# Two attention layers and their feed-forward parts on one Trainium2 core: the second attention's weighted sums in eight slots instead of nine

## The reference, cut to what matters

```python
x = L0(x, ctx)     # 8 heads of 16, then a relu feed-forward part
x = L1(x, ctx)     # 16 heads of 32; what follows is this layer
q  = layernorm(q_x, ...) @ Wq.T
kv = layernorm(kv_x, ...) @ Wkv.T
k, v = kv[0], kv[1]
attn = softmax(einsum('bhqd,bhkd->bhqk', q, k) * scale)
out  = einsum('bhqk,bhkd->bhqd', attn, v)
x = q_x + out @ Wo.T + bo
h = silu(x @ W1.T + b1)
x = x + h @ W2.T + b2
```

## Time and profile before

| | us |
|---|---|
| median of 3 runs (lowest, highest) | 5515.28 (5510.59, 5517.87) |
| the profiled execution's own time | 5516.99 |
| its span, first to last instruction | 5515.2 |
| PE busy in the span | 5316.3 (96%) |
| DVE busy | 4010.2 (73%) |
| ACT busy | 3172.4 (58%) |
| POOL busy | 2345.2 (43%) |

### The profile page before, as it was taken

How to read it: one execution, slowest core, us unless ns; L and a number is a source line. 1 busy time by engine, 2 the same in 40 slices (tenths; PEclk the granted TensorE clock), 3 DMA queues, 4 the chain that set the end, 5 groups by cost and what they waited for, 6 DMA issues and landing times. The chain is left out here.

```text
span 5515.2 us, 93900 instructions
## 1 busy us (share of the span) xinstructions
PE 5316.3 (96%) x28684; PEld 3344.6 (61%) x28684; DVE 4010.2 (73%) x6936; ACT 3172.4 (58%) x5792; POOL 2345.2 (43%) x1165
## 2 busy tenths in 40 slices
PE   8999999999799899999999999999999996999999
PEld 6744444444477565666666666656666663777777
DVE  6689999999477788888888888888888886332331
ACT  4268888888433466666666666666666663322222
POOL 0000000000000488888888888888888885000000
PEclk9989999999799899999999999999999998999999
DMA  7521111111333311111111111111111112322220
GB/s 216 130 48 38 38 38 38 38 38 31 111 120 115 101 40 30 41 39 42 41 28 41 41 42 40 28 42 41 39 42 28 41 28 62 120 87 69 92 84 23
DMA packets 329592, 324.44 MB, mean 59 GB/s; under 512 B 185744, under 2 KB 193808, under 8 KB 327184
## 3 DMA queue, kind: packets, MB, share of 16 engines
q1 hardware_dynamic: 329232, 319.92, 21.9%
HBM read 219.18 MB, written 100.53 MB: 58 GB/s over the span
## 5 line engine op out<-in xcount | busy, mean ns | idle before, releaser
L444 DVE TENSOR_REDUCE a_maxes<-a_mscore 128x1 f32<-128x458 f32 (+4 forms) x5376 | 3038.1, 624 | 590.5 <-PE a_mscore L502 559.1
L427 ACT ACTIVATE a_prob<-a_score 128x512 f32<-128x512 f32 x4992 | 2635.3, 598 | 1175.1 <-PE a_score L511 1162.1
L511 PE MATMUL a_score<-a_q,a_k 97*128 97x512 f32 (+1 forms) x4992 | 1980.2, 432 | 10.9 <-ACT a_prob L427 7.7
L502 PE MATMUL a_mscore<-a_k,a_qm 96*128 96x458 f32 (+4 forms) x5376 | 1893.1, 415 | 36.0 <-DMA a_k<-k 34.4
L530 PE MATMUL a_acc<-a_prob,a_v 128*32 128x512 f32 x9984 | 1601.0, 604 | 0.0
L502 PEld LDWEIGHTS a_mscore<-a_k,a_qm 96*128 96x128 f32 (+1 forms) x5376 | 1475.7, 310 | 159.9 <-DVE a_maxes L444 48.6
L393 POOL TENSOR_TENSOR a_added<-a_added,a_prob 128x1024 f32<-128x1024 f32 x640 | 1534.4, 2397 | 71.0
L511 PEld LDWEIGHTS a_score<-a_q,a_k 97*128 97x128 f32 (+1 forms) x4992 | 917.9, 193 | 970.7 <-ACT a_prob L427 525.5
L525 PE MATMUL a_acc<-a_prob,a_ones 128*1 128x512 f32 x2048 | 961.0, 591 | 0.0
L292 POOL MEMSET a_k<- 32x126 f32 (+4 forms) x6 | 6.3, 1053 | 1819.8 <-POOLq L60 1819.5
L530 PEld LDWEIGHTS a_acc<-a_prob,a_v 128*32 128x32 f32 x9984 | 292.5, 109 | 299.9 <-issue 154.7
(11 more groups left out here) (205 smaller groups left out, 3983.4 us busy)
## 6 DMA issues: line engine op xcount, KB each, us to landing
a_qm<-q SPq DMA_DIRECT2D x384, 64.0 KB, 1.9
a_q<-q SPq DMA_DIRECT2D x384, 64.0 KB, 1.9
acc<-a_acc_sb SPq DMA_DIRECT2D x384, 64.0 KB
e_part<-acc SPq DMA_DIRECT2D x90, 256.0 KB, 3.4
a_k<-k SPq DMA_DIRECT2D x48, 416.0 KB, 6.2
q<-m_qout SPq DMA_DIRECT2D x128, 128.0 KB, 2.3
e_wo<-wo_split SPq DMA_DIRECT2D x32, 512.0 KB, 4.3
k<-kv_k1out SPq DMA_DIRECT2D x24, 512.0 KB, 2.9
```

The source lines that it names most:

```text
L427: act.activation(prob[:, t], score[SCORES[it.j][t]][:], ACT.Exp, scale=SCALE).then_inc(exp_done, 1)
L444: dve.tensor_reduce(maxes[j][:, t, c:c + 1], mscore[u % UNIT_BANKS][:, 0:wide], AX.X, ALU.max).then_inc(unit_read, 1)
L502: pe.matmul(mscore[u % UNIT_BANKS][:, 0:wide], qm[j][r:r + ROW, t:NB:NB // P], kt[kk][r:r + ROW, at:at + wide], start=True, stop=True).the ...
L511: pe.matmul(score[SCORES[it.j][t]][:], kt[it.k][r:r + C, i * P:(i + 1) * P], qt[it.j][r:r + C, :], start=True, stop=True).then_inc(score_d ...
```

## The change

a1's tables are new. Tiles 0 to 7 fill two slots with values in all four column groups. Column group 3 of these two slots holds values, is copied out on its own (`side`, `copy_side` on ACT before exponential 20) and stored as a fourth partial result, so `SIDE` is 4. Six slots of three tiles each follow, whose column group 3 adds up the denominators of tiles 8, 9, 23 and 24, of the last tile (now all 128 rows, with ones only where there are keys), and `total`. That makes eight slots in four batches of two, in steps 17 and 22 of the item and in steps 9 and 13 of the next. DVE sums tiles 2 to 4 and 5 to 7, each in two pieces of 256 columns, in steps 9, 10, 17 and 19. POOL starts with tiles 10 and 11, adds both sums of DVE at once (1024 columns), and folds last. The table of units is new, and the weights are split from step 0 of the last item on. In `ending` each piece has three additions instead of two, the additions and splits for blocks 2 to 7 (counted from 0) are at other steps, piece 0 of a block is loaded one block earlier, and the last `attended` and `add_x` come one step later.

```diff
-            self.ROWS, self.SIDE, self.SUMS = 128, 3, 1
-            self.slots = [[(0, 3 * i), (1, 3 * i + 1), (2, 3 * i + 2), (3, ("one", 3 * i))] for i in range(8)]
-            self.slots.append([(0, 24), (1, 25), (3, ("sum", None))])
-            self.batches = [[0, 1], [2, 3], [4, 5], [6, 7], [8]]
-            self.at = {3: (3, True), 9: (4, True), 14: (0, False), 19: (1, False), 25: (2, False)}
-            self.copy_at = 5
+            self.ROWS, self.SIDE, self.SUMS = 128, 4, 1
+            self.slots = [[(c, 4 * i + c) for c in range(4)] for i in range(2)]
+            for i in range(2, 8):
+                first = 8 + 3 * (i - 2)
+                what = [("one", 8), ("one", 9), ("one", 23), ("one", 24), ("rest", 25), ("sum", None)][i - 2]
+                self.slots.append([(0, first), (1, first + 1), (2, first + 2), (3, what)])
+            self.batches = [[0, 1], [2, 3], [4, 5], [6, 7]]
+            self.at = {9: (2, True), 13: (3, True), 17: (0, False), 22: (1, False)}
+            self.copy_at, self.side_at = 14, 20
+            self.sum_at = (9, 10, 17, 19)
             self.CHUNKS, self.early = 7, 10
-            more = dict(enumerate([2, 1, 1, 0, 1, 2, 1, 1, 1, 0, 1, 2, 1, 1, 1, 1, 1, 2, 1, 1, 1, 1, 2, 1, 1, 0]))
+            more = dict(enumerate([1, 1, 1, 0, 2, 1, 2, 0, 1, 1, 2, 1, 1, 0, 1, 1, 2, 1, 2, 0, 2, 1, 1, 1, 2, 0]))
             self.FIRST, self.WIDTHS = [0], [SPAD]
...
-        self.closes = [max(ts) for ts in tiles]
+        summed = [[t[1] for i in b for _, t in self.slots[i] if isinstance(t, tuple) and t[0] != "sum"]
+                  for b in self.batches]
+        self.closes = [max(ts + ones) for ts, ones in zip(tiles, summed)]
...
-ADDS = 9
-ON_VECTOR, PIECES = range(22, 25), 4
-READ_BY = 7
+ADDS, READ_BY, SUMS_READ = 9, (1, 2, 5, 7), 8
+ON_VECTOR, PIECES = (range(2, 5), range(5, 8)), 2
+VSUMS = len(ON_VECTOR) * PIECES
...
-            ones = sb("ones", [P, 1], F32)
+            ones = sb("ones", [P, 2], F32)
             added, total = sb("added", [P, 2, NB], F32), sb("total", [P, NB], F32)
-            vsum = sb("vsum", [P, NB], F32)
+            vsum, side = sb("vsum", [P, 2, NB], F32), sb("side", [P, NB], F32)
...
-        SPLIT_AT = 4
+        SPLIT_AT = 0
...
-                for i in range(SIDE):
+                for i in range(ATEND):
                     sp.dma_start(acc_out[i, bass.ds(h * hd, hd), cols],
                                  acc_sb[j][i * 32:i * 32 + hd, :]).then_inc(acc_stored[j], 16)
+                if APART:
+                    sp.wait_ge(side_copied, n + 1)
+                    sp.dma_start(acc_out[ATEND, bass.ds(h * hd, hd), cols], side[3 * 32:P, :]).then_inc(side_stored, 16)
...
-                for i in range(1, 7):
-                    pool.wait_ge(exp_done, it.n * ST + 3 * i + 3)
-                    if i == 1:
+                for i, t in enumerate((10, 12, 14, 16, 18, 20)):
+                    pool.wait_ge(exp_done, it.n * ST + t + 2)
+                    if i == 0:
                         if not it.first:
                             pool.wait_ge(add_done, base)
-                        pool.tensor_tensor(added[:], prob[:, 1:3], prob[:, 4:6], ALU.add).then_inc(add_done, 1)
+                        pool.tensor_tensor(added[:], prob[:, 0:2], prob[:, 10:12], ALU.add).then_inc(add_done, 1)
                     else:
-                        pool.wait_ge(add_done, base + i - 1)
-                        pool.tensor_tensor(added[:], added[:], prob[:, 3 * i + 1:3 * i + 3],
-                                           ALU.add).then_inc(add_done, 1)
-                pool.wait_ge(exp_done, it.n * ST + ST)
+                        pool.wait_ge(add_done, base + i)
+                        pool.tensor_tensor(added[:], added[:], prob[:, t:t + 2], ALU.add).then_inc(add_done, 1)
+                pool.wait_ge(exp_done, it.n * ST + 23)
                 pool.wait_ge(add_done, base + 6)
-                pool.tensor_tensor(added[0:LAST_KEYS, 1], added[0:LAST_KEYS, 1], prob[0:LAST_KEYS, 25],
-                                   ALU.add).then_inc(add_done, 1)
+                pool.tensor_tensor(added[:, 0], added[:, 0], prob[:, 22], ALU.add).then_inc(add_done, 1)
+                pool.wait_ge(vsum_done, it.n * VSUMS + VSUMS)
                 pool.wait_ge(add_done, base + 7)
+                pool.tensor_tensor(added[:], added[:], vsum[:], ALU.add).then_inc(add_done, 1)
+                pool.wait_ge(add_done, base + 8)
                 if not it.first:
                     pool.wait_ge(pv_done, it.n * NBATCH)
                 pool.tensor_tensor(total[:], added[:, 0], added[:, 1], ALU.add).then_inc(add_done, 1)
-                pool.wait_ge(add_done, base + 8)
-                pool.wait_ge(vsum_done, it.n * PIECES + PIECES)
-                pool.tensor_tensor(total[:], total[:], vsum[:], ALU.add).then_inc(add_done, 1)
...
-                        last = min(max(L.batches[b][-1], 1), READ_BY - 1)
-                        act.wait_ge(add_done, it.n * ADDS - ADDS + (last if b < NBATCH - 1 else READ_BY))
-                if APART and t == ON_VECTOR[0] and not it.first:
-                    act.wait_ge(vsum_done, it.n * PIECES)
+                        act.wait_ge(add_done, it.n * ADDS - ADDS + READ_BY[b])
+                if APART and t == ON_VECTOR[0][0] and not it.first:
+                    act.wait_ge(vsum_done, it.n * VSUMS)
                 act.activation(prob[:, t], score[SCORES[it.j][t]][:], ACT.Exp, scale=SCALE).then_inc(exp_done, 1)
+            def copy_side(n):
+                act.wait_ge(pv_done, n * NBATCH + 1)
+                act.wait_ge(side_stored, n * 16)
+                act.activation(side[3 * 32:P, :], acc[3 * 32:P, :], ACT.Copy).then_inc(side_copied, 1)
             for it in items(act):
-                for s in range(GROUPS):
-                    if s == L.copy_at and not it.first:
+                for t in range(ST):
+                    if t == L.copy_at and not it.first:
                         copy_acc(it.n - 1, 1 - it.j, it.prev_use)
-                    exp(it, 2 * s)
-                    exp(it, 2 * s + 1)
+                    if APART and t == L.side_at:
+                        copy_side(it.n)
+                    exp(it, t)
...
-                    dve.wait_ge(exp_done, n * ST + ON_VECTOR[-1] + 1)
-                    dve.wait_ge(add_done, n * ADDS)
+                    dve.wait_ge(exp_done, n * ST + tiles[-1] + 1)
+                    if which == 0 and not first:
+                        dve.wait_ge(add_done, n * ADDS - ADDS + SUMS_READ)
                 cols = slice(i * NB // PIECES, (i + 1) * NB // PIECES)
-                dve.tensor_reduce(vsum[:, cols], prob[:, ON_VECTOR[0]:ON_VECTOR[-1] + 1, cols].rearrange("p t c -> p c t"),
+                dve.tensor_reduce(vsum[:, which, cols], prob[:, tiles[0]:tiles[-1] + 1, cols].rearrange("p t c -> p c t"),
...
-                    if APART and t < PIECES and not it.first:
-                        add_up(it.n - 1, t)
-                if APART and it.last:
-                    for i in range(PIECES):
-                        add_up(it.n, i)
+                    if APART and t in L.sum_at:
+                        add_up(it.n, it.first, *divmod(L.sum_at.index(t), PIECES))
...
+                if b == 1 and APART:
+                    pe.wait_ge(side_copied, n + 1)
...
+                            col = 1 if what[0] == "rest" else 0
...
-    SUM_AT, HALF_AT, A_AT, ADD_AT = (1, 3, 5, 7), (2, 4, 6, 8), (10, 11, 12, 13), (11, 12, 13, 14)
+    SUM_AT = [(1, 3, 5, 7)] + [(0, 3, 6, 9)] * (BLOCKS - 1)
+    HALF_AT = [(2, 4, 6, 8)] + [(1, 4, 7, 10)] * (BLOCKS - 1)
+    A_AT, ADD_AT = (11, 12, 13, 14), (12, 13, 14, 15)
...
-                    for k in range(KT) if n > 0 else ():
+                    for k in range(1, KT) if n > 0 else ():
                         next_acc(n + 1, k)
                     for d in range(KT):
                         load_wo(n + 1, d)
+                if n + 2 < BLOCKS:
+                    next_acc(n + 2, 0)
...
```

52 lines of the change are left out of this document (32 added, 20 removed).

## The result

The changed kernel takes 5428.08 us (median of 4 runs, 5424.27 to 5431.30), the kernel before 5512.93 in 4 runs beside it (5502.76 to 5517.87). The ratio is 0.9848, with a 95% interval of 0.9831 to 0.9865: 85 us faster. The prediction said 5410, in a range of 5375 to 5455.

A forecast was written before the change was run, and what follows sets the result against it. PE bounds a1: 21.66 - 1.20 - 0.18 + 0.52 = 20.80 us an item. 126 x 0.86 = 108.4, first item 1 more, a1's end costing 4, `ending` giving 0.5: 106 us less, 5410, range 5375 to 5455.

The forecast's parts named there:

- One batch less: In each a1 item, dropping the single-slot batch saves 1.20 us, and two waits ahead of it another 0.18.
- The long run: In a1, 13 scores and units between the batches of steps 22 and 9: bank waits start score 9 0.52 us late.
- The item: One a1 item goes from 21.66 to 20.80 us, a gain of 0.86.
- DVE and POOL: In an a1 item, sums of 0.95 us give DVE 19.0 us of work; POOL's 20.6 fits by 0.2.
- rival (c): In a1, DVE's sums slow POOL's additions as the splits do: item 22.2 us, 5590 us in all; chance 0.07.
- (a): In a1, the 13-score run waits for nothing and POOL's 20.6 us sets the item: 5382 us; chance 0.13.
- (b): In a1, the 13-score run goes at DVE's pace, losing 0.9 us: item 21.15 us, 5453 us; chance 0.15.
- (d): In a1, the wait only shifts, the seam losing three times 0.52 us: nothing gained, about 5515 us; chance 0.05.
- The end of a1: From item 126's first exponential to POOL's last addition: 59.2 us instead of 55.1, 4 us more.
- `ending`: After a1: 10.3 us gained from six waits, 5 lost at seven seams, 4.8 in its opening; net 0.5 gained.
- The first item: In a1, the first item has no old batches to finish and gives 1 us more gain.
- The opening: Start of the ending code: one more addition of 0.71 us and one more load for each of four pieces, 4.8 lost.

The follow-up runs named there:

- experiment 2: The changed kernel with its second batch cut in two, so five batches for the eight slots, slot 3 alone at step 25: 5431.46 us, ratio 0.9852.
- experiment 4: The changed kernel without the matmuls that add up the denominators of tiles 8, 9, 23, 24 and 25: 5420.47 us, ratio 0.9833.
- experiment 1: The changed kernel with a1's score banks reordered in odd items, so score 0 takes the bank of score 23, not 24: 5405.08 us, ratio 0.9803.
- experiments 5 and 6: The changed kernel, ending's code alone altered: additions of blocks 2 to 7 one step earlier (5412.02 us), or tables and load order as before the change (5445.60 us).

## Why the prediction was right, point by point

**One batch less** (1.20 an item). In the mean over all items of the kernel before, the single-slot batch lies in 1.30 us from score to score. The prediction took off 0.21 for the two scores without it, but 0.21 is a score behind a unit; a score right behind a score starts 0.235 later. With the 0.10 for the slower start the batch was worth 1.16. The two waits ahead of it cost 0.175 (predicted 0.18). The split of the 1.16 matters: 0.87 is the slot, and the 0.29 for the batch is mostly taken back by ACT (experiment 2). That a matmul in the fourth column group costs nothing beside the others is shown (experiment 4), and so is that values there cost what ones do: the batch of step 17, with values in all four groups, adds 1.95 us to its step, and the three others 1.93 to 1.94.

**The long run** (0.52). The mechanism was right, and the sum came out by luck: its terms were wrong both ways. Score 9 comes 6.06 us after score 23 in the mean, 5.54 of them PE's own pace (counted from the same gaps where nothing waits), so 0.52 are lost, as predicted. But score 0 waits 0.25 and not 0.35, since it starts 0.10 behind the exponential that frees its bank and not 0.15, and score 4 waits 0.08 and not 0.17. Left out was the slower start of PE behind each of the two waits, 0.34 from score to unit instead of 0.24, which the prediction had counted behind batches: 0.19 for both.

**The item** (20.80, measured 20.893). The missing 0.09 is 12 of the 18 us by which the prediction missed. 0.04 of it are the batch's price and the waits ahead of it, above. Another 0.04 lie in the new table of units, which the prediction put at nothing: two more steps than before have no unit and two more have two. Two scores are 0.235 apart without a unit between them, 0.447 with one and 0.68 with two, so each such pair of steps takes 0.02 longer than two steps with one unit each (the means of score-to-score times in steps without a wait).

**DVE and POOL.** The sums are 0.94 apart (1.03 long), predicted 0.95. DVE kept up. POOL's pause is 0.7 where I had 0.2, since its additions follow each other more closely (2.47) than I took; its work of an item is 20.2 us, not 20.6. They kept their 2.39 beside sums, as at 2913.27, where this row of DVE starts together with POOL's addition shown above, and in the mean of the page's group (the last number but the wait):

```profile
2913.27 1.03 DVE L482 TENSOR_REDUCE a_vsum<-a_prob 128x256 f32<-128x768 f32 x1
...
L410 POOL TENSOR_TENSOR a_added<-a_added,a_prob 128x1024 f32<-128x1024 f32 x640 | 1533.7, 2396 | 71.0
```

So rival (c) is refuted: what the split does to POOL a reduction doesn't do. The rule of the Trainium skill that the prediction cited ("SBUF — State Buffer", Who interferes with whom), that a `tensor_reduce` never contends with GpSimd, agrees with this trace, at 2.39 us beside the sum.

**The rivals.** (a) wanted the long run free of waits: with the seam's gone it still took 5.90 (experiment 1), and POOL still paused. (b) wanted DVE as the pace of it; no row shows PE waiting for DVE in the run. (d) is refuted by the result. None of the kernels brought the item down to POOL's own work.

**The end of a1.** 59.2 was predicted and 59.2 measured, again with two small errors that cancel: POOL starts 8.0 us into the item and works 51.2, which with two items of 20.2 leaves 10.8 for DVE's splits (predicted 10.1, with items of 20.6). The short additions suffered too: 3.14 us for the one of 512 columns at 4519.86, where it takes 1.28 in the steady part.

**`ending`.** The six old waits are gone. They had made a block 102.35 us long, where one without waits takes 100.39: 11.8 in all (predicted 10.3). The seams cost 5.5 (predicted 5). Not foreseen was block 0, whose additions keep their old steps: a wait of 1.0 for `e_hl`, and 6.0 us at half the clock behind the opening's wait where the kernel before had 3.4, 1.3 us more. The opening cost 5.6 (predicted 4.8); the nine kernels of the experiments that have the same code there took 46.4 to 48.0 us for it, so that difference is within their scatter. Together -2.1 instead of +0.5.

**The first item** gained nothing: it lost 2.1 where I had counted a gain of 1.9. PE waits 0.65 for maxima in it, with DVE's sums in the way, and the clock fell; see below. The kernels of experiments 5 and 6 have the same code in a1, the clock didn't fall there, and it took 21.1 us: the clock's part is 1.8, and even without it the item is 0.3 longer than before.

**Ahead of a1** the -1.9 is scatter. Kernels with the same code up to there began a1's exponentials between 1854.1 and 1862.3 us, and between 1843.6 and 1846.1 where a0's last item kept its clock.

## What to carry to other kernels

When a stage is bound by one engine, price a removed piece by what it makes the next engine do: the slot was worth its 0.87 us, but of the 0.3 for switching only 0.07 was left, since ACT had used those pauses. Count the slower start behind every wait that you predict, not only behind the ones that you remove, and take the mean over many items where single items differ. And place optional work of a nearly full engine under the pauses that the bound engine's other work makes; two sums in the wrong steps cost 0.64 us an item here, nearly as much as the whole change gained.
